# Attention kernel on one NeuronCore: the block maxima turned on VectorE in 32x32 squares, the group statistics summed as fp32r records, and GpSimd held at two places

## The chip, the cores and the metric

The kernel runs on one core of a Trainium2 chip. The metric is the device time of one execution in microseconds (us), lower is better. The kernel before was timed three times; its median is 1215.44 us (1214.12 to 1215.74).

## The reference, cut to what matters

The input x has 16 images of 64x64 positions and 256 channels (n = 4096 positions per image). Every operation is in float32.

```python
xg  = group_norm(x)                      # 32 groups of 8 channels, eps 1e-5
qkv = xg @ W_qkv                         # 256 -> 768, split in q, k, v
k   = softmax(k, over the 4096 positions)
ctx = einsum('bdn,ben->bde', k, v)       # 256 x 256
out = einsum('bde,bdn->ben', ctx, q)
y   = x + out @ W_out + b_out
```

The softmax runs over the positions of an image, so it needs a maximum for each of the 256 channels of k.

## The kernel before, in words

The work goes image by image, b = 0 to 15, and an image in 8 chunks j of 512 positions; a chunk has 4 tiles of 128 positions. `n` is b + 1. Each float32 product is made of three fp32r products: every operand is split in a rounded part (`_hi`, written by ScalarE) and a rest (`_lo`, a subtraction on VectorE or GpSimd).

For one image the program does this.
- **Statistics.** `bn_half` (VectorE, L849) reads chunks of the image after the next; `bn_sum` (L851) gives mean and variance of each channel. `stats_mean` (TensorE, L462) multiplies the 128 means by `grp`, a 128x128 matrix of 1/8 inside each group of 8 channels, in float32; `mean_of` (VectorE, L860 to L865) subtracts, and forms each channel's share of the variance; `stats_var` (L466) sums that with the same matrix; `var_of` (L871) adds eps; `rstd_of` (GpSimd, L357) takes the power -0.5. These small steps for image n are placed in the first two steps of the gather of image b.
- **Keys.** `keys` (L399) makes `ps_k` for each chunk; `keys_out` (ScalarE, L685) copies it to `e_raw`; `key_max` (VectorE, L889 and L892) keeps in `mx` [128 x 256] the maximum over tiles, of one block of four chunks (blk 0: j = 0 to 3; blk 1: j = 4 to 7). A row of `mx` is a position modulo 128, a column a channel.
- **The maximum of a block.** `turn_max` (TensorE, L447) transposes the two halves of `mx` into PSUM; `block_max` (VectorE, L901) reduces them to `m_blk` [128 x 2], a channel in each partition; `spread_max` (TensorE, L455) multiplies `m_blk`, broadcast along 128 columns, by the identity in float32, which puts the 256 maxima in every partition of PSUM; `shift` (VectorE, L917) subtracts them from `e_raw`. `block_scales` (L906, L909) gives `dm`, the difference of the block's maximum to that of the image, and ScalarE takes its exponential, `alpha`.
- **Exponentials and gather.** `exps` (ScalarE, L693 and L699) makes `e_hi` and the exact exponential, `e_low` (VectorE, L924) the rest. `gather_high` (TensorE, L480 and L482: 16 matmuls) and `gather_low` (L492: 8) multiply chunk j of the exponentials by the chunk of x.
- **Combine and emit.** `combine_u`, `combine_m` and `bias_sum` (L542) form one 256x256 matrix and a bias; `emit` (L564, L573) applies it to all chunks of x of the image, between the `keys` of image n.

The order on every engine is written out by hand, one queue each. TensorE begins the gather of image b with `gather_high(b, 0)`, then `turn_max(b, 1)`, `stats_mean(n)`, `gather_low(b, 0)`, `gather_high(b, 1)`, `spread_max(b, 1)`, `stats_var(n)`, `gather_low(b, 1)` (L619 to L628; in image 0 the two statistics come after the gathers of chunks 3 and 4). For block 0 of image n, `turn_max(n, 0)` and `spread_max(n, 0)` stand around `keys(n, 4)` (L661 to L666). VectorE's order is in `gather_steps` (L1053) and in `period` (L1100 to L1121). GpSimd (L372) makes `xt_lo` (`xt_low`, L341) and `x_lo` (`x_low`, L347), each 128x1024, as soon as ScalarE has the rounded part; the first of a period is `xt_low(n, 0)`.

Two places in the code that the prediction speaks of:

```python
# VectorE, before: gather_steps
block_max(b, 1)
if more:
    mean_of(n, np_)
block_scales(b)
```

```python
# GpSimd, before: the start of a period
if more:
    xt_low(n, np_, 0)
    if b:
        rstd_of(n, np_)
for j in range(HALF, NCH):
    x_low(b, j)
```

## Time and profile before

| | |
|---|---|
| median of three runs | 1215.44 us |
| the profiled execution | 1214.93 us, its span 1213.2 us |
| TensorE (PE) busy | 1190.1 us, 98% of the span |
| VectorE (DVE), ScalarE (ACT), GpSimd (POOL) busy | 69%, 69%, 51% |
| granted TensorE clock | 1.00 throughout |
| data moved by DMA | 219 GB/s over the span |

The span is cut from the first to the last instruction; 1.7 us of the execution lie outside it. A matmul row of the timeline shows when the first of a group starts and how long the group runs to its modelled end; matmuls are pipelined, so what one costs is read from the distance of starts, not from its duration. PE is TensorE, DVE VectorE, ACT ScalarE, POOL GpSimd.

### The profile page before, as it was taken

The page shows a single profiled execution, that of the slowest core. Times are in us where ns is not written, and L with a number is a line of the kernel's source. Part 1 is how long each engine was busy: PE and PEld are TensorE (multiplying, and loading weights), DVE is VectorE, ACT ScalarE, POOL GpSimd, SP SyncE. Part 2 cuts the span into 40 slices and gives each one's busy share as a digit, 9 for nine tenths or more (in the row PEclk, how much of TensorE's full clock was granted, in tenths as well). Part 3 has the DMA queues.
Part 4 walks back from the last instruction along what each step waited for, and adds up shares of the span by engine and source line. Part 5 has one row for each costly group of instructions (what it writes and reads, how often), then busy time and mean ns, then how long its engine had stood idle before and what let it go on. Part 6 is the DMA issues. An engine that isn't in the chain of part 4 may idle for free.

```text
span 1213.2 us, 21447 instructions
## 1 busy us (share of the span) xinstructions
PE 1190.1 (98%) x8460; PEld 1115.8 (92%) x8460; DVE 842.1 (69%) x1582; ACT 840.1 (69%) x1140; POOL 622.4 (51%) x288
## 2 busy tenths in 40 slices
PE   4999999999999999999999999999999999999998
PEld 4998999999899998999989999899999989999897
DVE  6877667676776767768776677766767676676551
ACT  5767768677685776757677686776857768577664
POOL 8664564635645355563655636356463564536520
PEclk9999999999999999999999999999999999999999
DMA  9448666576765758666486665867657576573524
GB/s 339 146 167 294 218 235 205 195 269 208 274 203 199 264 172 294 226 206 237 162 301 229 221 227 183 286 209 252 204 201 263 193 278 225 201 252 122 191 74 170
DMA packets 107077, 266.71 MB, mean 220 GB/s; under 512 B 10208, under 2 KB 10208, under 8 KB 106976
## 3 DMA queue, kind: packets, MB, share of 16 engines
q1 hardware_dynamic: 106976, 265.33, 63.5%
q8 instruction: 67, 1.10, 0.4%
q14 instruction: 34, 0.28, 0.1%
HBM read 198.18 MB, written 67.11 MB: 219 GB/s over the span
## 4 chain that ended last, share of the span: by engine, by line
PE 93%; DVE 2%; ACT 1%; POOL 1%; DMA 1%; issue 1%; SPq 0%; DVEq 0%; POOLq 0%; ACTq 0%
PE ps_k L399 29%; PE ps_e L564 19%; PE ps_e L573 10%; PE ps_g L492 5%; PE ps_e L480 5%; PE ps_e L492 5%; PE ps_e L482 5%; PE ps_g L480 4%; PE ps_g L482 4%; PE ps_g L511 1%; PE ps_g L528 1%; PE ps_g L542 1%; PE ps_g L534 1%; POOL x_lo L347 1%; DVE mx L892 1%
## 5 line engine op out<-in xcount | busy, mean ns | idle before, releaser
L341 POOL TENSOR_TENSOR xt_lo<-xt_raw,xt_hi 128x1024 fp32r<-128x1024 f32 x128 | 307.4, 2404 | 434.5 <-ACT xt_hi L676 309.1
L347 POOL TENSOR_TENSOR x_lo<-x_raw,x_hi 128x1024 fp32r<-128x1024 f32 x128 | 281.4, 2216 | 65.6 <-ACT x_hi L681 56.2
L892 DVE TENSOR_TENSOR mx<-ps_k,mx 128x256 f32<-128x256 f32 x480 | 203.3, 424 | 95.8 <-ACT e_raw L685 74.3
L733 ACT ACTIVATE o_stage<-ps_e,bias 128x512 f32<-128x512 f32 x253 | 170.9, 689 | 114.1 <-PE ps_e L573 114.1
L399 PE MATMUL ps_k<-wk_hi,xt_hi 128*128 128x256 f32 x1024 | 207.1, 284 | 1.0 <-DVE mx L892 0.7
L399 PE MATMUL ps_k<-wk_lo,xt_hi 128*128 128x256 f32 x1024 | 205.5, 283 | 0.0
L685 ACT ACTIVATE e_raw<-ps_k 128x512 f32<-128x512 f32 x256 | 141.4, 596 | 87.2 <-PE ps_k L399 87.2
L849 DVE BATCH_NORM_STATS2 bn<-xs 128x6 f32<-128x512 f32 x240 | 154.5, 686 | 40.7 <-DMA xs<-in_xt_dram 39.5
L693 ACT ACTIVATE e_hi<-e_raw 128x1024 fp32r<-128x1024 f32 x128 | 135.1, 1055 | 60.9 <-DVE e_raw L917 33.0
L399 PEld LDWEIGHTS ps_k<-wk_hi,xt_hi 128*128 128x128 f32 x1024 | 163.4, 190 | 8.7 <-issue 1.8
L399 PE MATMUL ps_k<-wk_hi,xt_lo 128*128 128x256 f32 x1024 | 158.2, 283 | 0.0
L399 PEld LDWEIGHTS ps_k<-wk_lo,xt_hi 128*128 128x128 f32 x1024 | 157.4, 189 | 0.0
L564 PE MATMUL ps_e<-xt_hi,acc_hi 128*128 128x512 f32 x474 | 150.3, 398 | 0.0
L573 PE MATMUL ps_e<-xt_hi,u_lo 128*128 128x512 f32 x474 | 150.2, 398 | 0.0
L564 PE MATMUL ps_e<-xt_lo,acc_hi 128*128 128x512 f32 x474 | 148.8, 395 | 0.0
L681 ACT ACTIVATE x_hi<-x_raw 128x1024 fp32r<-128x1024 f32 x128 | 134.5, 1050 | 11.4 <-DMA x_raw<-in_xn_dram 11.2
L676 ACT ACTIVATE xt_hi<-xt_raw 128x1024 fp32r<-128x1024 f32 x128 | 135.0, 1055 | 3.8 <-DMA xt_raw<-in_xt_dram 3.8
L399 PEld LDWEIGHTS ps_k<-wk_hi,xt_lo 128*128 128x128 f32 x1024 | 137.3, 189 | 0.0
L480 PE MATMUL ps_e<-x_hi,e_hi 128*128 128x258 f32 x512 | 125.8, 283 | 0.7 <-POOL x_lo L347 0.7
L482 PE MATMUL ps_e<-x_lo,e_hi 128*128 128x256 f32 x512 | 125.5, 282 | 0.0
L482 PE MATMUL ps_g<-x_lo,e_hi 128*128 128x256 f32 x512 | 124.8, 281 | 0.0
L480 PE MATMUL ps_g<-x_hi,e_hi 128*128 128x258 f32 x512 | 124.8, 282 | 0.0
(129 smaller groups left out, 1992.7 us busy)
## 6 DMA issues: line engine op xcount, KB each, us to landing
xt_raw<-in_xt_dram SPq DMA_DIRECT2D x128, 512.0 KB, 4.3
x_raw<-in_xn_dram SPq DMA_DIRECT2D x128, 512.0 KB, 3.5
out_dram<-o_stage SPq DMA_DIRECT2D x127, 512.0 KB, 4.5
xs<-in_xt_dram SPq DMA_DIRECT2D x240, 256.0 KB, 5.1
w_setup<-in_w_dram SPq DMA_DIRECT2D x2, 256.0 KB, 10.1
out_dram<-o_stage SPq DMA_DIRECT2D x2, 256.0 KB, 2.0
wk<-in_w_dram SPq DMA_DIRECT2D x1, 256.0 KB, 9.9
wq_t<-in_w_dram SPq DMA_DIRECT2D x1, 256.0 KB, 10.9
```

The costliest lines, as they stand in the source:

```text
L341: nc.gpsimd.tensor_tensor(xt_lo[:, s], xt_raw[:, s], xt_hi[:, s].bitcast(F32), ALU.subtract).then_inc(xt_lo_ready, 1)
L347: nc.gpsimd.tensor_tensor(x_lo[:, s], x_raw[:, s], x_hi[:, s, :, 0:C].bitcast(F32), ALU.subtract).then_inc(x_lo_ready, 1)
L399: return nc.tensor.matmul(ps_k[:, j % 2, t // 2, (t % 2) * C:(t % 2 + 1) * C], (xt_hi, xt_lo)[xs_][:, slot(j, parity), c, t * P:(t + 1) * ...
L480: nc.tensor.matmul(ps_g[j // HALF][:, d, 0:C + 2], w_, x_hi[:, j % X_SLOTS, t, :], start=(j % HALF == 0 and t == 0), stop=False, skip_grou ...
L482: nc.tensor.matmul(ps_g[j // HALF][:, d, 0:C], w_, x_lo[:, j % X_SLOTS, t, :], start=False, stop=False, skip_group_check=True)
L564: nc.tensor.matmul(out_psum(b, u, h), hi[:, c, h * P:(h + 1) * P], x_[:, s, c, :], start=(n == 0 and c == 0), stop=False, skip_group_check ...
L573: last = nc.tensor.matmul(out_psum(b, u, h), lo[:, c, h * P:(h + 1) * P], xt_hi[:, s, c, :], start=False, stop=(c == CB - 1), skip_group_c ...
L685: nc.scalar.activation(e_raw[:, j, 2 * h:2 * h + 2, :].rearrange("p t c -> p (t c)"), ps_k[:, j % 2, h, :], ACT.Copy).then_inc(k_out, 1)
L693: nc.scalar.activation(e_hi[:, j % E_SLOTS], e_raw[:, j], ACT.Exp).then_inc(e_hi_ready, 1)
L733: nc.scalar.activation(o_stage[:, u % O_SLOTS, h, :], src, ACT.Identity, bias=bias[:, h:h + 1]).then_inc(o_ready, 1)
L849: nc.vector.bn_stats(bn[:, q % CB, q // CB, :], xs[:, q % S_SLOTS, :]).then_inc(bn_done, 1)
L892: nc.vector.tensor_tensor(mx[:], tile, mx[:], ALU.max).then_inc(max_done, 1)
```

## The change

- VectorE turns `mx` with its own transpose, which works in squares of 32x32 (`turned`). A reduction over each square's 32 columns gives `quad` [128 x 8]; three moves bring the other three groups of 32 partitions beside the first; a last reduction gives `m_blk`, now 32 partitions x 8. `turn_max` is gone from TensorE. The moves are written as a `tensor_reduce` of single elements (`move`), not as copies.
- `block_diag` (VectorE) splits `m_blk` in a rounded part and a rest in `m_parts` (64 partitions), and multiplies it by two stacked 32x32 identities into `diag`, 64x256 fp32r. `spread_max` is now one fp32r matmul of 256 columns with ones as weights.
- The group sums of images 1 to 15 use `grp_r` and parts (rounded, rest) in fp32r: one matmul of 4 columns in place of a float32 one of 2. VectorE forms the parts (`mean_parts`, `var_parts`) and adds the two sums afterwards. In `mean_of`, `dev` is now the sum of `mv` and `neg_mean`, both in SBUF; before, it read the mean from PSUM.
- `alpha` is made from 32 partitions (`alpha_q`) and spread by four moves in `spread_scales`.
- GpSimd waits for `diag_ready` of block 1 before `xt_low(n, 0)`, and for that of block 0 before `xt_low(n, 5)`.
- ScalarE makes the fp32r copies of `grp` and of the ones, and `eye2`, before its first work.

```diff
             def period(b, parity, more, more2):
                 n, np_ = b + 1, 1 - parity
+                pool.wait_ge(diag_ready, b * 2 + 2)
                 if more:
                     xt_low(n, np_, 0)
...
                     for j in range(3, NCH):
+                        if j == HALF + 1:
+                            pool.wait_ge(diag_ready, n * 2 + 1)
                         xt_low(n, np_, j)
...
-            def turn_max(b, blk):
-
-                to = max_psum(b, blk)
-                pe.wait_ge(max_done, b * (TILES * NCH) + TILES * HALF * (blk + 1))
-                for d in range(CB):
-                    last = nc.tensor.transpose(to[:, 0, d * P:(d + 1) * P], mx[:, d * P:(d + 1) * P], ident)
-                last.then_inc(t_ps, 1)
-
             def spread_max(b, blk):
-                to = max_psum(b, blk)
-                pe.wait_ge(m_blk_ready, b * 2 + (blk + 1))
-                for d in range(CB):
-                    last = nc.tensor.matmul(to[:, 1, d * P:(d + 1) * P],
-                                            m_blk[:, blk, d:d + 1].broadcast_to([P, P]), ident,
-                                            start=(d == 0), stop=True, skip_group_check=True)
-                last.then_inc(bc_ps, 1)
+                pe.wait_ge(diag_ready, b * 2 + (blk + 1))
+                nc.tensor.matmul(max_psum(b, blk)[:, 1, 0:C], one_r[0:2 * Q].broadcast_to([2 * Q, P]), diag,
+                                 start=True, stop=True).then_inc(bc_ps, 1)
...
+                    pe.wait_ge(mean_parts_ready, b)
+                    nc.tensor.matmul(stats_psum(b, 0), grp_r[:], mean_parts[:].rearrange("p k c -> p (k c)"), start=True,
+                                     stop=True).then_inc(mean_ps, 1)
...
+                    pe.wait_ge(var_parts_ready, b)
+                    nc.tensor.matmul(stats_psum(b, 1), grp_r[:], var_parts[:].rearrange("p k c -> p (k c)"), start=True,
+                                     stop=True).then_inc(var_ps, 1)
...
             def mean_of(b, parity):
                 dve.wait_ge(mean_ps, b + 1)
...
+                    nc.vector.tensor_scalar(mean_rest[:], sums[:, CB:2 * CB], -1.0, None,
+                                            ALU.mult).then_inc(mean_rest_ready, 1)
+                    dve.wait_ge(mean_rest_ready, b)
+                    nc.vector.scalar_tensor_tensor(out=neg_mean[:, parity, :], in0=sums[:, 0:CB], scalar=-1.0,
+                                                   in1=mean_rest[:], op0=ALU.mult, op1=ALU.add).then_inc(mean_sum_ready, 1)
+                    dve.wait_ge(mean_sum_ready, b)
+                    nc.vector.tensor_tensor(dev[:], mv[:, :, 0], neg_mean[:, parity, :], ALU.add).then_inc(mean_read, 1)
...
+                if b > 0:
+                    dve.wait_ge(var2_ready, b + 1)
+                    move(var_parts[:, 0, :], var2[:]).then_inc(var_hi_ready, 1)
+                    dve.wait_ge(var_hi_ready, b)
+                    nc.vector.tensor_tensor(var_parts[:, 1, :], var2[:], var_parts[:, 0, :].bitcast(F32),
+                                            ALU.subtract).then_inc(var_parts_ready, 1)
...
             def block_max(b, blk):
-                src = max_psum(b, blk)
-                dve.wait_ge(t_ps, b * 2 + (blk + 1))
-                nc.vector.tensor_reduce(m_blk[:, blk, :], src[:, 0, 0:C].rearrange("p (d n) -> p d n", d=CB),
-                                        AX_X, ALU.max).then_inc(m_blk_ready, 1)
+                n = b * 2 + blk + 1
+                dve.wait_ge(max_done, n * (TILES * HALF))
+                nc.vector.transpose(turned[:], mx[:]).then_inc(turned_ready, 1)
+                dve.wait_ge(turned_ready, n)
+                nc.vector.tensor_reduce(quad[:, :, 0], turned[:].rearrange("p (q k) -> p q k", k=Q), AX_X,
+                                        ALU.max).then_inc(quad_ready, 1)
+                dve.wait_ge(quad_ready, n)
+                for r in range(1, QUADS):
+                    last = move(quad[0:Q, :, r], quad[r * Q:(r + 1) * Q, :, 0])
+                last.then_inc(quad_moved, 1)
+                dve.wait_ge(quad_moved, n)
+                nc.vector.tensor_reduce(m_blk[:, blk, :], quad[0:Q], AX_X, ALU.max).then_inc(m_blk_ready, 1)
+
+            def block_diag(b, blk):
+                n = b * 2 + blk + 1
+                dve.wait_ge(m_blk_ready, n)
+                move(m_parts[0:Q, :], m_blk[:, blk, :]).then_inc(m_part_hi_ready, 1)
+                dve.wait_ge(m_part_hi_ready, n)
+                nc.vector.tensor_tensor(m_parts[Q:2 * Q, :], m_blk[:, blk, :], m_parts[0:Q, :].bitcast(F32),
+                                        ALU.subtract).then_inc(m_part_lo_ready, 1)
...
+                dve.wait_ge(m_part_lo_ready, n)
+                nc.vector.tensor_tensor(diag.rearrange("p (q k) -> p q k", k=Q),
+                                        eye2[:].unsqueeze(1).broadcast_to([2 * Q, NQ, Q]),
+                                        m_parts[:].bitcast(F32).unsqueeze(2).broadcast_to([2 * Q, NQ, Q]),
+                                        ALU.mult).then_inc(diag_ready, 1)
```

TensorE at the start of the gather of an image (b from 1 to 14), the 16 matmuls of `gather_high` on either side left out. Before:

```order
L447 MATMUL ps_k<-zero_eye,mx 128x128 x2
L462 MATMUL ps_k<-mv,grp 128x2
...
L455 MATMUL ps_k<-zero_eye,m_blk 128x128 x2
L466 MATMUL ps_k<-var,grp 128x2
```

And changed:

```order
L499 MATMUL ps_k<-mean_parts,grp_r 128x4
...
L488 MATMUL ps_k<-u_hi,one_r 128x256
L509 MATMUL ps_k<-var_parts,grp_r 128x4
```

The positions are the same, the two transposes are gone, and each float32 matmul has become one fp32r matmul (`u_hi` is the memory that `diag` lies in).

VectorE at the same place, from the last `e_low` ahead of the gather to the first `shift` of block 1. Before:

```order
L924 TENSOR_TENSOR e_lo<-e_raw,e_hi 128x1024
L901 TENSOR_REDUCE m_blk<-ps_k 128x2
L860 TENSOR_TENSOR dev<-mv,ps_k 128x2
L861 TENSOR_SCALAR neg_mean<-ps_k 128x2
L865 TENSOR_SCALAR var<-dev,mv 128x1 x2
L906 TENSOR_REDUCE m_all<-m_blk 128x2
L909 TENSOR_TENSOR dm<-m_blk,m_all 128x4
L961 TENSOR_TENSOR b_mean<-b_col,neg_mean 128x2
L917 TENSOR_TENSOR e_raw<-e_raw,ps_k 128x1024
```

And changed, up to `dm`:

```order
L985 STREAM_TRANSPOSE turned<-mx 128x256
L987 TENSOR_REDUCE quad<-turned 128x8
L890 TENSOR_REDUCE quad<-quad 32x8 x3
L994 TENSOR_REDUCE m_blk<-quad 32x8
L890 TENSOR_REDUCE m_parts<-m_blk 32x8
L1001 TENSOR_TENSOR m_parts<-m_blk,m_parts 32x8
L1006 TENSOR_TENSOR u_hi<-eye,m_parts 64x256
L924 TENSOR_SCALAR mean_rest<-ps_k 128x2
L927 SCALAR_TENSOR_TENSOR neg_mean<-ps_k,mean_rest 128x2
L930 TENSOR_TENSOR dev<-mv,neg_mean 128x2
L933 TENSOR_SCALAR var<-dev,mv 128x1 x2
L890 TENSOR_REDUCE var_parts<-var 128x2
```

One instruction ahead of `mean_of` has become nine, and the chain from the mean to the part that `stats_var` reads has grown from four instructions to seven; the last of them (L940, `var_parts`) and `dm` follow.

## Rows read from the trace of the kernel before

**Rows 1.** The page, busy time of each engine over the span.
```profile
PE 1190.1 (98%) x8460; PEld 1115.8 (92%) x8460; DVE 842.1 (69%) x1582; ACT 840.1 (69%) x1140; POOL 622.4 (51%) x288
```
**Rows 2.** What TensorE waited for: total us, times, longest.
```profile
PE ps_k L447 <- DVE mx L892: 1.9, 2, 1.6
...
PE ps_e L480 <- POOL x_lo L347: 0.7, 2, 0.4
```
**Rows 3.** Timeline of PE, start of image 1's gather: start us, us, operation, count.
```profile
123.21 0.28 PE L480 MATMUL ps_g<-x_hi,e_hi 128*128 128x258 f32 x1
...
125.12 0.38 PE L447 MATMUL ps_k<-zero_eye,mx 128*128 128x128 f32 x2
...
128.44 0.60 PE L455 MATMUL ps_k<-zero_eye,m_blk 128*128 128x128 f32 x4
...
130.08 0.28 PE L480 MATMUL ps_g<-x_hi,e_hi 128*128 128x258 f32 x1
...
132.95 0.28 PE L480 MATMUL ps_g<-x_hi,e_hi 128*128 128x258 f32 x1
```
**Rows 4.** Timeline of PE, around `keys(2, 4)`, and `keys(2, 3)` before it.
```profile
168.75 0.40 PE L399 MATMUL ps_k<-wk_hi,xt_hi 128*128 128x256 f32 x2
...
172.10 0.63 PE L564 MATMUL ps_e<-xt_lo,acc_hi 128*128 128x512 f32 x2
...
174.43 0.38 PE L447 MATMUL ps_g<-zero_eye,mx 128*128 128x128 f32 x2
...
177.49 0.61 PE L455 MATMUL ps_g<-zero_eye,m_blk 128*128 128x128 f32 x4
...
178.41 0.63 PE L564 MATMUL ps_e<-xt_lo,acc_hi 128*128 128x512 f32 x2
```
**Rows 5.** PE groups by form: `bias_sum`'s records, 128 of one column.
```profile
L542 PE MATMUL ps_g<-neg_mean,acc 128*128 128x1 f32 x128 | 15.2, 239 | 0.0
```
**Rows 6.** Timeline of DVE at the start of image 1's gather.
```profile
122.62 1.21 DVE L924 TENSOR_TENSOR e_lo<-e_raw,e_hi 128x1024 fp32r<-128x1024 f32 x1
...
125.95 0.15 DVE L861 TENSOR_SCALAR neg_mean<-ps_k 128x2 f32<-128x2 f32 x1
126.14 0.46 DVE L865 TENSOR_SCALAR var<-dev,mv 128x1 f32<-128x1 f32 x2
...
126.69 0.85 DVE L909 TENSOR_TENSOR dm<-m_blk,m_all 128x4 f32<-128x4 f32 x1
```
**Rows 7.** DVE groups by form, one operation over 256 columns.
```profile
L889 DVE COPY mx<-ps_k 128x256 f32<-128x256 f32 x32 | 13.5, 421 | 2.4 <-PE ps_e L447 1.4 <-ACT e_raw L685 1.0
...
L901 DVE TENSOR_REDUCE m_blk<-ps_k 128x2 f32<-128x256 f32 x16 | 6.8, 424 | 23.9 <-PE ps_k L447 23.9
```
**Rows 8.** Timeline of POOL at the start of image 1's gather.
```profile
125.12 2.40 POOL L341 TENSOR_TENSOR xt_lo<-xt_raw,xt_hi 128x1024 fp32r<-128x1024 f32 x1 [7.79 <-ACT xt_hi L676]
```
**Rows 9.** Line L909 (`dm`): duration ns min/median/max of its 16.
```profile
L909 DVE TENSOR_TENSOR dm<-m_blk,m_all x16: 161/833/849, 52.0 to 1158.7; 128x4 f32<-128x4 f32 x16
```
**Rows 10.** Timeline of DVE, the maxima of `keys(2, 3)`.
```profile
171.98 1.87 DVE L892 TENSOR_TENSOR mx<-ps_k,mx 128x256 f32<-128x256 f32 x4 [2.79 <-ACT e_raw L685]
```
**Rows 11.** Timeline of POOL beside it.
```profile
173.46 2.42 POOL L341 TENSOR_TENSOR xt_lo<-xt_raw,xt_hi 128x1024 fp32r<-128x1024 f32 x1 [3.19 <-ACT xt_hi L676]
```
**Rows 12.** Timeline of POOL, image 0: two `first_e_low`.
```profile
49.88 4.77 POOL L352 TENSOR_TENSOR e_lo<-e_raw,e_hi 128x1024 fp32r<-128x1024 f32 x2 [1.43 <-ACT e_raw L699]
```
**Rows 13.** Timeline of DVE, image 0: `shift(0, 3)` and `e_low(0, 3)`.
```profile
50.24 1.21 DVE L917 TENSOR_TENSOR e_raw<-e_raw,ps_e 128x1024 f32<-128x1024 f32 x1
...
55.31 2.79 DVE L924 TENSOR_TENSOR e_lo<-e_raw,e_hi 128x1024 fp32r<-128x1024 f32 x1
```
**Rows 14.** Timeline of PE, image 0: `spread_max(0, 1)`.
```profile
53.53 0.60 PE L455 MATMUL ps_k<-zero_eye,m_blk 128*128 128x128 f32 x4
```
**Rows 15.** Timeline of DVE, image 15: the last `e_low` before its gather.
```profile
1156.95 1.22 DVE L924 TENSOR_TENSOR e_lo<-e_raw,e_hi 128x1024 fp32r<-128x1024 f32 x1
```
**Rows 16.** Timeline of PE, image 15: `gather_low(15, 1)`, behind `spread_max(15, 1)`.
```profile
1160.60 1.21 PE L492 MATMUL ps_g<-x_hi,e_lo 128*128 128x258 f32 x8
```

More of the change, by code:

```diff
@@ L29 @@
 POOL_LOW = 3
+Q = 32
+QUADS = P // Q
 def build(nc: bass.Bass, xt: bass.AP, xn: bass.AP, w: bass.AP, b_out: bass.AP, out: bass.AP):
@@ L93, in build @@
         eye = [zero_eye[:, P:3 * P], zero_eye[:, 0:2 * P]]
-        grp = sb("grp", [P, P])
+        with nc.sbuf_tensor("grp", [P, P], F32) as grp:
+            pass
+        grp_r = sb("grp_r", [P, P], F32R)
+        one_r = sb("one_r", [P, 1], F32R)
+        var_sum = sb("var_sum", [P, CB])
+        var_parts = sb("var_parts", [P, 2, CB], F32R)
+        mean_parts = sb("mean_parts", [P, 2, CB], F32R)
+        mean_rest = sb("mean_rest", [P, CB])
         mx = sb("mx", [P, C])
@@ L107, in build @@
         u_lo = sb("u_lo", [P, CB, C], F32R)
+        with nc.sbuf_tensor("turned", [P, C], F32) as turned:
+            pass
         u_hi = sb("u_hi", [P, CB, C], F32R)
+        diag = u_hi[0:2 * Q, 1, :]
         m_lo = u_lo
@@ L213, in stats_psum @@
         def stats_psum(b, which):
-            return ps_k[:, 0, 0, C + which * CB:C + (which + 1) * CB] if b == 1 else ps_k[:, 1, which, 0:CB]
+            if b == 1:
+                return ps_k[:, 0, 0, C + 2 * CB * which:C + 2 * CB * (which + 1)]
+            return ps_k[:, 1, which, 0:CB if b == 0 else 2 * CB]
         def max_psum(b, blk):
@@ new lines, in stats_mean @@
+            def stats_mean(b):
+                if b == 0:
+                    pe.wait_ge(mv_ready, 1)
+                    nc.tensor.matmul(stats_psum(b, 0), grp_r[:].bitcast(F32), mv[:, :, 0], start=True,
+                                     stop=True).then_inc(mean_ps, 1)
+                else:
+                    pe.wait_ge(max_done, b * (TILES * NCH))
+                    pe.wait_ge(mean_parts_ready, b)
+                    nc.tensor.matmul(stats_psum(b, 0), grp_r[:], mean_parts[:].rearrange("p k c -> p (k c)"), start=True,
+                                     stop=True).then_inc(mean_ps, 1)
@@ new lines, in stats_var @@
+            def stats_var(b):
+                if b == 0:
+                    pe.wait_ge(var2_ready, 1)
+                    nc.tensor.matmul(stats_psum(b, 1), grp_r[:].bitcast(F32), var2[:], start=True,
+                                     stop=True).then_inc(var_ps, 1)
+                else:
+                    pe.wait_ge(var_parts_ready, b)
+                    nc.tensor.matmul(stats_psum(b, 1), grp_r[:], var_parts[:].rearrange("p k c -> p (k c)"), start=True,
+                                     stop=True).then_inc(var_ps, 1)
@@ L739, in emit @@
                         emit_half(b, u, h)
+            act.wait_ge(consts_ready, 5)
+            nc.scalar.activation(grp_r[:], grp[:], ACT.Copy).then_inc(grp_r_ready, 1)
+            nc.scalar.activation(one_r[:], one_col[:], ACT.Copy).then_inc(one_r_ready, 1)
+            for r in range(2):
+                last = nc.scalar.activation(eye2[r * Q:(r + 1) * Q, :], ident[r * Q:(r + 1) * Q, r * Q:(r + 1) * Q],
+                                            ACT.Copy)
+            last.then_inc(eye2_ready, 1)
             for j in range(NCH):
@@ L908, in block_scales, with spread_scales @@
                 dve.wait_ge(m_all_ready, b + 1)
-                nc.vector.tensor_tensor(dm[:], m_blk[:], m_all[:].unsqueeze(1).broadcast_to([P, 2, CB]),
+                nc.vector.tensor_tensor(dm[:], m_blk[:], m_all[:].unsqueeze(1).broadcast_to([Q, 2, NQ]),
                                         ALU.subtract).then_inc(dm_ready, 1)
+            def spread_scales(b):
+                dve.wait_ge(alpha_q_ready, b + 1)
+                by_quad = alpha_q[:].rearrange("p k (d r) -> p k d r", r=QUADS)
+                for r in range(QUADS):
+                    last = move(alpha[r * Q:(r + 1) * Q, :, :], by_quad[:, :, :, r])
+                last.then_inc(alpha_ready, 1)
             def shift(b, j):
@@ L1020, in _ @@
             bn_half(1, 10)
+            block_max(0, 0)
+            block_diag(0, 0)
             key_maxes(0, 4)
-            block_max(0, 0)
             bn_half(1, 11)
@@ L1044, in first_gather @@
                 mean_of(1, 1)
+                spread_scales(0)
                 take_first(0)
@@ L1055, in gather_steps @@
                 block_max(b, 1)
+                block_diag(b, 1)
                 if more:
@@ L1065, in gather_steps @@
                 e_low(b, 4)
+                spread_scales(b)
                 take_first(b)
```

73 lines of the change are left out of this document (55 added, 18 removed).

## Prediction

> **What bounds the kernel now.** I read the page's busy times first: TensorE is busy 98% of the span, the next engines 69% [rows 1]. Then its waits: it waited for no engine for longer than 1.6 us at once, and in the steady images it did not wait at all; the waits that I use lie in images 0, 1 and 15 [rows 2]. So matmul time taken away shortens the span one for one, as long as nothing that TensorE waits for becomes late. What can become late is on VectorE and GpSimd, so I read last the timelines of the places where the change works. The reader is to see there when VectorE has a result, and when TensorE comes for it.
>
> **What TensorE loses.** Each price is a distance between starts. At the start of a gather, from `gather_high(b, 0)` at 123.21 to `gather_high(b, 2)` at 130.08 are 6.87 us. One chunk with nothing between is 132.95 - 130.08 = 2.87 us, two are 5.74, so turn, mean, spread and variance cost 1.13 us [rows 3]. They become three matmuls. A record of one column in `bias_sum` costs 15.2 / 128 = 0.12 us [rows 5], and a full one in `gather_high` (123.21 to 125.12, 16 of them) also 0.12 [rows 3]; three are 0.36. Saved: 0.77 us. At block 0, turn to the second emit row are 178.41 - 174.43 = 3.98 us, the same work without turn and spread 172.10 - 168.75 = 3.35 [rows 4]: 0.63 us become 0.12, saved 0.51. Images 1 to 14 have the first place with statistics, images 1 to 15 the second: 14 x 0.77 + 15 x 0.51 = **18.4 us off**. Images 0 and 15 are counted below.
>
> **What VectorE gets, at the start of a gather.** Its work there begins when the last `e_low` is out, 122.62 + 1.21 = 123.8 [rows 6]. The turn, the reduction and the product for `diag` have 256 columns each, 0.42 us, and 0.03 more before the next can start: 1.35 us. I have no row of a transpose; the copy and the reduction of the same size agree [rows 7], the ends are 0.35 and 0.9. Six small ones remain (three moves, the last maximum, rounded part, rest). A small one that depends on the one before starts 0.19 us after it (125.95, then 126.14) [rows 6]; two independent small ones start 0.07 apart. The moves are independent, but each reads another quarter of the partitions, so I give them the long distance: six at 0.18 are 1.08, and 0.85 if the moves overlap. `diag` is ready at 123.8 + 2.43 = 126.2. TensorE, 0.2 us earlier without the turn, comes for it after chunk 0, the mean and the first 16 of chunk 1, at 123.21 + 2.87 + 0.12 + 1.91 = 128.1, so `spread_max` is covered by 1.9 us.
>
> The Trainium skill (VectorE: DVE Perf Modes, section on two Vector instructions with no wait between them) says that an instruction starts only after all earlier ones if its input begins in another quadrant of partitions than the last one read. By that rule the moves cannot overlap and `diag` is at 126.2; by the short distance it would be at 126.0 and the sum 3 us lower.
>
> **The wait that comes in its place.** `dm` has four columns and takes 0.16 us at the least, but 0.83 in the median [rows 9]. In image 1 it starts at 126.69 and ends at 127.54; GpSimd's `xt_low(n, 0)` runs from 125.12 to 127.52 [rows 6, 8]. In image 0 `e_low(0, 3)` takes 2.79 us for 1.21, under GpSimd as well [rows 13]. Both have two SBUF inputs. `neg_mean` and the variance steps, with PSUM or one tensor, ran at normal length in the same window [rows 6]. So a VectorE operation with two SBUF inputs stands still until GpSimd's instruction ends. Before the change `dev` read PSUM and escaped this. Now `dev` and the rest for `var_parts` have two SBUF inputs each. And the new wait releases `xt_low(n, 0)`, whose input is ready at 125.1 [rows 8], just when `diag` is ready: it runs from 126.3 to 128.7, while `dev` comes 0.5 us after `diag`. `dev` ends at 128.7, the two variance steps take 0.50, rounded part and rest 0.36, the signal 0.04: `var_parts` at 129.6. TensorE comes for it behind the spread at 128.1 + 0.12 = 128.2. It stands 1.4 us, and the whole queue behind it. If `dev` slips in before GpSimd, the rest is caught instead and the wait is 1.0; with overlapping moves 1.1; with a turn of 0.9 us 1.8. Fourteen images: **19.6 us on** (14.0 to 25).
>
> After that nothing more is late: by the same distances `shift(b, 4)` follows 0.8 us later than before and TensorE itself 0.5, and the 0.3 between them is covered by the two chunks of gather that lie ahead of the first use (2 x 2.87 us); without them it would be added to the wait. `spread_scales` (four moves, 0.7 us at most) stands where VectorE waits for the gather of chunk 3; were that wait gone, the first copy of the sums would be 0.7 us later.
>
> **Block 0.** The maxima end at 171.98 + 1.87 = 173.85 [rows 10]. GpSimd's `xt_low(2, 4)` runs until 175.88 [rows 11] and holds the rest for `m_parts` until then, which is due two big and five small distances after the maxima, at 175.65; `diag` is at 176.5, TensorE comes at 177.49 - 0.18 = 177.3 [rows 4]. No cost. The hold of `xt_low(n, 5)` moves it to 176.6, and `keys(2, 5)` stand behind the next emit: nothing.
>
> **Image 0.** `shift(0, 3)` ends at 51.45 [rows 13]; the chain reaches the rest at 53.25, where the second `first_e_low` holds it until 49.88 + 4.77 = 54.65 [rows 12]. `diag` is at 55.3, `spread_max(0, 1)` stood at 53.53 [rows 14]: 1.7 us late. Then `xt_low(1, 0)` starts and holds `dm`, and `shift(0, 4)`, the remaining `bn_half` and `mean_parts` are 4 to 5 us late; followed through the queues this adds up to 5.5 us on TensorE's queue by chunk 7, 2 if `dm` slips in first. I take **4.5 us on**. The fills of ScalarE at the start fit in its wait for the first data, and block 0 there costs at most 0.3.
>
> **Image 15.** The last emits stand elsewhere, so TensorE comes early. `e_low` ends at 1158.17 [rows 15], `diag` 2.4 later at 1160.6, when `gather_low(15, 1)` started before [rows 16]: no gain, no loss.
>
> **Sum.** -18.4 + 19.6 + 4.5 = +5.7 us on the profiled execution of 1214.93, that is 1220.6 us; against the median, which is 0.5 higher, the same change would give 1221.1. I say 1220.5.
>
> **The rivals.**
> - *VectorE's small operations are not held.* If the 0.83 of `dm` had another cause, `var_parts` would come seven small distances after `diag`, at 127.5, and be hidden behind TensorE's 128.2. Only image 0 costs 1 to 2 us. 1214.9 - 18.4 + 1.5 = 1198. For it: nothing but that the rows show just two operations held. Against it: both ends agree with GpSimd's to 0.02 us.
> - *The wait is short.* Overlapping moves, `dev` ahead of GpSimd and image 0 at 2 us: 1214.9 - 18.4 + 14 x 0.9 + 2 = 1211. It decides as soon as the wait per image is below 1.15 us, where faster begins.
> - *Block 0 is late too.* If the transpose or the reduction is also held by GpSimd, the chain at block 0 starts at 175.9, `diag` is at 178.3, and TensorE stands 1.0 us in 15 images: 1235. The trace has no transpose; operations with one tensor, as the variance steps in the window of [rows 8], were not held [rows 6], so I give this little.
> - *The hold does nothing.* If GpSimd's input came later than `diag`, the new waits would be idle; here it is ready 1.1 us earlier, so they act.
>
> **How the numbers follow.** My forecast, with its own range of 1214 to 1227, has 0.57. Unheld operations have 0.13, the short wait 0.17, block 0 late 0.09, anything else 0.04. The range 1206 to 1229 leaves out the first rival and most of the third, and takes in the second with both ends of the moves. A change under 0.2% (2.4 us) could not be told from none. Faster (below 1213.0): the first two rivals and a little of the rest, 0.32. Same: the low end of my case, 0.16. Slower: 0.52.
>
> **What the changed profile would show.** TensorE's waits would have a new first line, `stats_var`'s matmul waiting for VectorE's L940 some 14 times with 1.4 us each. `dev` (L930) would last until GpSimd's `xt_low` ends, 2.2 us in place of 0.15. `spread_max` would wait only in images 0 and 15. TensorE's span between the gathers of two images would stay near 74.0 us, 1.3 less in matmuls and as much more in waits. I am wrong if L930 has its normal length, or if `spread_max` waits in every image.

## The result, and the profile after

The changed kernel takes 1228.64 us (median of 4 runs, 1227.95 to 1229.39) against 1215.44 for the one before (median of three; a fourth run of it took 4129.46 us and is left out): the ratio is 1.0112, with an interval from 1.0092 to 1.0131. It is slower by 13 us, where the prediction said 5. The profiled execution has a span of 1226.8 us, 13.6 more than before, and all further sums are made on the spans.

The page's busy line of the changed kernel, against [rows 1]:

```profile
PE 1183.1 (96%) x8270; PEld 1102.2 (90%) x8270; DVE 940.4 (77%) x1992; ACT 842.0 (69%) x1144; POOL 621.6 (51%) x288
```

TensorE lost 7.0 us of busy time and 190 instructions, and yet the span grew. VectorE is busy for 98 us more; part of this is standing still, as the timeline below shows.

What TensorE waited for in the changed kernel (total us, times, longest):

```profile
PE ps_k L509 <- DVE var_parts L940: 15.6, 14, 1.1
PE ps_k L488 <- DVE u_hi L1006: 4.4, 2, 3.5
```

The first row is new: 14 waits of 1.1 us at `stats_var`. The second has an unusual longest wait, 3.5 us, in image 0. Before, the longest for this block maximum was 1.6 us, at `turn_max` [rows 2].

The timeline of VectorE at the start of image 1's gather, to be held against [rows 6]:

```profile
128.94 1.22 DVE L1039 TENSOR_TENSOR e_lo<-e_raw,e_hi 128x1024 fp32r<-128x1024 f32 x1
130.08 0.43 DVE L985 STREAM_TRANSPOSE turned<-mx 128x256 f32<-128x256 f32 x1
130.55 0.42 DVE L987 TENSOR_REDUCE quad<-turned 128x8 f32<-128x256 f32 x1
131.00 0.50 DVE L890 TENSOR_REDUCE quad<-quad 32x8 f32<-32x8 f32 x3
...
131.93 0.16 DVE L1001 TENSOR_TENSOR m_parts<-m_blk,m_parts 32x8 fp32r<-32x8 f32 x1
132.12 0.42 DVE L1006 TENSOR_TENSOR u_hi<-eye,m_parts 64x256 fp32r<-64x256 f32 x1
...
132.64 0.16 DVE L927 SCALAR_TENSOR_TENSOR neg_mean<-ps_k,mean_rest 128x2 f32<-128x2 f32 x1
132.84 2.20 DVE L930 TENSOR_TENSOR dev<-mv,neg_mean 128x2 f32<-128x2 f32 x1
135.07 0.46 DVE L933 TENSOR_SCALAR var<-dev,mv 128x1 f32<-128x1 f32 x2
135.56 0.15 DVE L890 TENSOR_REDUCE var_parts<-var 128x2 fp32r<-128x2 f32 x1
135.75 0.16 DVE L940 TENSOR_TENSOR var_parts<-var,var_parts 128x2 fp32r<-128x2 f32 x1
```

And of GpSimd beside it, against [rows 8]:

```profile
132.62 2.40 POOL L381 TENSOR_TENSOR xt_lo<-xt_raw,xt_hi 128x1024 fp32r<-128x1024 f32 x1 [8.93 <-DVE u_hi L1006]
```

The chain from the end of `e_low` (130.16) to that of `diag` (132.54) takes 2.4 us. GpSimd starts at 132.62, 0.08 us behind `diag`. `dev`, of two columns, starts at 132.84 and ends at 135.04, and GpSimd's operation ends at 135.02. `neg_mean` (L927) also has two tensors, but one lies in PSUM: it ran in 0.16 us, although it started at 132.64, 0.02 us behind GpSimd. The kernel before shows this more plainly: its `dev`, with one tensor in PSUM, started 0.76 us behind GpSimd [rows 8] in image 1, and all 16 of them, each under an operation of GpSimd, took 0.15 to 0.16 us.

```profile
125.88 0.15 DVE L860 TENSOR_TENSOR dev<-mv,ps_k 128x2 f32<-128x2 f32 x1
```

The variance steps, the rounded part and the rest follow at normal length.

The timeline of TensorE at the same place, against [rows 3]:

```profile
129.50 0.28 PE L524 MATMUL ps_g<-x_hi,e_hi 128*128 128x258 f32 x1
...
131.39 0.17 PE L499 MATMUL ps_k<-mean_parts,grp_r 128*128 128x4 f32 x1
...
134.47 0.38 PE L488 MATMUL ps_k<-u_hi,one_r 64*128 64x256 f32 x1
135.97 0.27 PE L509 MATMUL ps_k<-var_parts,grp_r 128*128 128x4 f32 x1 [1.12 <-DVE var_parts L940]
...
137.14 0.28 PE L524 MATMUL ps_g<-x_hi,e_hi 128*128 128x258 f32 x1
```

From `gather_high(1, 0)` at 129.50 to `gather_high(1, 2)` at 137.14 are 7.64 us, before 6.87. The wait of 1.12 us took more than the 0.77 that was saved.

The timeline of TensorE around the spread of block 0, from `keys(2, 4)` at 180.84 to the second emit row at 184.66, against [rows 4]:

```profile
180.84 0.39 PE L442 MATMUL ps_k<-wk_hi,xt_hi 128*128 128x256 f32 x2
...
182.73 1.11 PE L442 MATMUL ps_k<-wk_hi,xt_lo 128*128 128x256 f32 x8
183.77 0.38 PE L488 MATMUL ps_g<-u_hi,one_r 64*128 64x256 f32 x1
184.08 0.74 PE L608 MATMUL ps_e<-xt_hi,acc_hi 128*128 128x512 f32 x2
184.66 0.62 PE L608 MATMUL ps_e<-xt_lo,acc_hi 128*128 128x512 f32 x2
```

The whole is 3.82 us long. Without any spread it was 3.35, so `spread_max` costs 0.47 us here. The float32 turn and spread together cost 0.63.

**Where the 13.6 us are.** I cut the spans at the matmul of `stats_mean` at the start of a gather (125.34 before, 131.39 after). Thirteen images further on it is at 1087.14 and at 1099.61. This gives three pieces: 6.1 us up to the first cut, 6.4 us in the thirteen images, 1.1 us behind them. The median distance of one image grew from 73.94 to 74.45 us.

Within an image, two places changed, and in each kernel each of them takes the same time in all images to 0.03 us. At the start of a gather (first matmul of chunk 0 to that of chunk 2, 14 images) the median was 6.85 us and is 7.64. At block 0 (the last emit row ahead of `keys(n, 4)` to the second one behind the spread, 15 images) it was 4.44 and is 4.29.

Of the 6.1 us, 1.0 lies ahead of image 0's `stats_mean` (15.33 before, 16.35 after) and 4.6 between it and that of image 1. The first is a DMA chunk that landed late; of the experiments, two started at 15.5 and the others at 16.0 to 16.6, so these runs cannot tell it from chance. The second is image 0. Two views show it, first VectorE's timeline:

```profile
54.60 1.38 DVE L1001 TENSOR_TENSOR m_parts<-m_blk,m_parts 32x8 fp32r<-32x8 f32 x1
56.02 0.42 DVE L1006 TENSOR_TENSOR u_hi<-eye,m_parts 64x256 fp32r<-64x256 f32 x1
...
56.55 2.36 DVE L1016 TENSOR_TENSOR dm<-m_blk,m_all 32x16 f32<-32x16 f32 x1
```

and TensorE's `spread_max(0, 1)`, which stood at 53.53 before [rows 14]:

```profile
56.49 0.58 PE L488 MATMUL ps_k<-u_hi,one_r 64*128 64x256 f32 x1 [3.47 <-DVE u_hi L1006]
```

The granted clock changed here as well. The windows of the changed kernel behind this wait (us; busy time of PE, PEld, DVE, ACT, POOL; then the granted TensorE clock, DMA share, GB/s).

```profile
56.00:58.00 2.00, 1.51 (x5) 1.28 (x6) 1.94 (x3) 1.80 (x2) 1.48 (x1) 0.50 0.00 0
58.00:60.00 2.00, 2.00 (x12) 2.00 (x11) 2.00 (x4) 0.21 (x1) 2.00 (x2) 0.50 0.00 0
60.00:62.00 2.00, 2.00 (x11) 2.00 (x11) 2.00 (x3) 0.67 (x1) 1.04 (x1) 0.50 0.72 262
62.00:64.00 2.00, 2.00 (x16) 2.00 (x16) 1.96 (x6) 2.00 (x3) 0.00 (x0) 0.83 0.00 0
```

TensorE stood for 3.47 us, from 53.0 to 56.5, and its granted clock was 0.50, the 1.2 GHz level, from 55.9 to 62.7. Before, the same stretch has 1.00 throughout.

### The profile page after: what moved, and what is told of

The parts are those of the page before. It is cut to its first block, busy times and chain, and to the rows that moved or that the text cites. A ratio compares the mean times of both kernels' runs of the same rounds, so it can differ in the third digit from the quotient of the medians.

```text
span 1226.8 us, 21528 instructions
## 1 busy us (share of the span) xinstructions
PE 1183.1 (96%) x8270; PEld 1102.2 (90%) x8270; DVE 940.4 (77%) x1992; ACT 842.0 (69%) x1144; POOL 621.6 (51%) x288
## 4 chain that ended last, share of the span: by engine, by line
PE 78%; DVE 13%; ACT 4%; DMA 2%; issue 1%; POOL 1%; SPq 0%; DVEq 0%; POOLq 0%; ACTq 0%
PE ps_k L442 24%; PE ps_e L608 17%; PE ps_e L617 9%; PE ps_e L524 5%; PE ps_e L536 5%; PE ps_e L526 5%; PE ps_g L536 4%; DVE mx L974 3%; DVE dev L930 3%; PE ps_g L524 2%; PE ps_g L526 2%; DVE e_lo L1039 2%; DMA xs<-in_xt_dram 1%; ACT e_raw L741 1%; PE ps_g L555 1%
## 6 DMA issues: line engine op xcount, KB each, us to landing
wq_t<-in_w_dram SPq DMA_DIRECT2D x1, 256.0 KB, 11.1
```

## The experiments

All of them start from the changed kernel. Each was timed beside the kernel before on the same chip (1215.4, 1215.5, 1215.1 and 1214.8 us in the four sets). "Per image" is the median distance between the cuts defined above (73.94 before, 74.45 after), "thirteen" the sum of the thirteen (961.8 and 968.2).

### The wait at the variance

Theory: `dev` stands under GpSimd, and this makes the 14 waits. Its alternative: the chain is long because it has more instructions. **Pointer operand** leaves all steps, but gives `dev` and the rest of `var_parts` one tensor and a per-partition scalar in place of two tensors. That makes two instructions of each, so the chain becomes longer, not shorter.

```diff
-nc.vector.tensor_tensor(dev[:], mv[:, :, 0], neg_mean[:, parity, :], ALU.add)
+for c in range(CB):
+    last = nc.vector.tensor_scalar(dev[:, c:c + 1], mv[:, c, 0:1], neg_mean[:, parity, c:c + 1], None, ALU.add)
```

(the same for the subtraction that writes `var_parts[:, 1]`)

> The changed kernel with dev and the rest of var_parts formed as subtractions with a per-partition scalar, two instructions of one column in place of one with two SBUF tensors. Theory 'GpSimd holds the operation with two SBUF tensors': dev takes 0.15 us per column in place of 2.20, TensorE no longer waits for var_parts (15.6 us of waits gone, and with the restart about 1.2 us in each of 14 images), so about 17 us less than the changed kernel: 1211 to 1213 us. Rival 'the chain itself is too long, the held operation only uses slack': the wait shrinks by less than half, 1220 us or more.

Measured: 1214.21 us, ratio 0.9995 (0.9986 to 1.0005), 73.27 per image. Its groups on VectorE (busy us, mean ns) and TensorE's wait at the variance:

```profile
L931 DVE TENSOR_SCALAR dev<-mv,neg_mean 128x1 f32<-128x1 f32 x30 | 5.0, 210 | 0.5
L944 DVE TENSOR_SCALAR var_parts<-var,var_parts 128x1 fp32r<-128x1 f32 x30 | 5.0, 210 | 0.5
```

```profile
PE ps_k L509 <- DVE var_parts L944: 0.4, 1, 0.4
```

The time is 1.2 us above the range that was expected. Neither operation is held now, the wait is down from 15.6 us to 0.4, and 14.4 us are gone from the median. The number of instructions was not the cause. The gain against before is 0.67 us per image, about half of the 1.28 that the prediction counted.

**Float32 statistics** undoes the other half of the change instead: `grp` and the sums in float32, no parts, `dev` reading PSUM again; the transposes in squares, the diagonal and GpSimd's waits stay.

```diff
-    pe.wait_ge(mean_parts_ready, b)
-    nc.tensor.matmul(stats_psum(b, 0), grp_r[:], mean_parts[:].rearrange("p k c -> p (k c)"), start=True, stop=True)
+    pe.wait_ge(mv_ready, b + 1)
+    nc.tensor.matmul(stats_psum(b, 0)[:, 0:CB], grp_r[:].bitcast(F32), mv[:, :, 0], start=True, stop=True)
```

(in sense; likewise for the variance and for VectorE's side)

> The changed kernel with the group statistics undone: float32 matmuls of two columns, dev read from PSUM, no parts; the maxima on VectorE, the diagonal and GpSimd's waits stay. Theory 'the fp32r statistics are what brought the held operations': no wait for the variance, two float32 records cost 0.2 us more than two fp32r ones, so a steady image at 73.4 to 73.6 us and about 1215 us, 13 us less than the changed kernel. Rival 'the held operation is not the point, the longer VectorE chain at the diagonal is': the wait for the variance stays above 0.8 us and the time above 1222 us.

Measured: 1214.48 us, ratio 0.9990 (0.9980 to 0.9999), 73.52 per image. TensorE no longer waits at the variance of any image but the first. `dev` has one operand in PSUM again and, without the two steps ahead of it, starts at 129.79 in image 1, 0.15 us before GpSimd. Its group:

```profile
L923 DVE TENSOR_TENSOR dev<-mv,ps_k 128x2 f32<-128x2 f32 x16 | 2.3, 143 | 0.7 <-PE ps_k L496 0.7
```

So there are two ways out of the wait with the same result, and the fp32r records themselves are worth 73.52 - 73.27 = 0.25 us per image.

### What the spread costs

The changed `spread_max` is a matmul over 64 rows (`64*128` in its row) among others over 128. Theory: the change of shape costs time. Rivals: fetching the new weights, or the arithmetic of 256 columns. **Spread over 128 rows** fills the diagonal, `m_parts` and `eye2` up with zeros, so the sum is the same and the matmul has the shape of its neighbours.

```diff
-diag = u_hi[0:2 * Q, 1, :]
+diag = u_hi[:, 1, :]
-nc.tensor.matmul(max_psum(b, blk)[:, 1, 0:C], one_r[0:2 * Q].broadcast_to([2 * Q, P]), diag,
+nc.tensor.matmul(max_psum(b, blk)[:, 1, 0:C], one_r[:].broadcast_to([P, P]), diag,
```

> The changed kernel with the spread matmul over 128 rows in place of 64 (the added 64 rows of the diagonal are zero, the same VectorE instruction writes them). Theory 'a matmul of 64 rows among those of 128 costs extra because the array changes its shape': the distance keys(n, 4) to the second emit row falls from 3.82 us to about 3.5, 15 times 0.3 at block 0, while at block 1 the wait for var_parts takes back what is gained: about 1224 us. Rival 'a matmul with broadcast ones as weights or 256 columns of the diagonal is dear in itself': no change, 1228.6 us.

TensorE's timeline at the spread of block 0 of image 2, where in the changed kernel 1.04 us lay ahead of the spread's start and 0.89 behind it, up to the second emit row:

```profile
183.92 1.11 PE L442 MATMUL ps_k<-wk_hi,xt_lo 128*128 128x256 f32 x8
184.87 0.28 PE L488 MATMUL ps_g<-u_hi,one_r 128*128 128x256 f32 x1
184.99 0.62 PE L608 MATMUL ps_e<-xt_hi,acc_hi 128*128 128x512 f32 x2
185.45 0.62 PE L608 MATMUL ps_e<-xt_lo,acc_hi 128*128 128x512 f32 x2
```

Here it is 0.95 and 0.58 us, together 0.40 less, and over 15 images block 0 takes 3.89 us in place of 4.29. With twice the rows the matmul became cheaper. Yet the whole kernel is hardly faster: 1225.99 us, ratio 1.0083 (1.0066 to 1.0100). The wait at the variance took up what was gained at the start of a gather:

```profile
PE ps_k L509 <- DVE var_parts L942: 18.8, 15, 1.4
```

It was 15.6 us, 1.1 at the most; the start of a gather takes 7.66 us, as before this edit 7.64. The saving at block 0 shows in the median image, 74.08, but four of the thirteen took 75.0 to 75.5, and in this run TensorE waited four times, 3.7 us in all, for ScalarE's `o_stage`, which the changed kernel never did.

**Spread twice** issues the same 64-row matmul a second time right behind itself.

```diff
+nc.tensor.matmul(max_psum(b, blk)[:, 1, 0:C], one_r[0:2 * Q].broadcast_to([2 * Q, P]), diag,
+                 start=True, stop=True)
```

> The changed kernel with the spread matmul of 64 rows issued twice in a row (the second overwrites the first with the same values). Theory 'change of shape': the second one needs no change and adds 0.12 to 0.2 us at block 0, about 2 us in all, 1231 us. Rival 'dear in itself': each adds 0.3 to 0.45 us, 15 times at block 0, 1233 to 1236 us.

```profile
182.76 1.11 PE L442 MATMUL ps_k<-wk_hi,xt_lo 128*128 128x256 f32 x8
183.79 0.38 PE L488 MATMUL ps_g<-u_hi,one_r 64*128 64x256 f32 x1
184.01 0.28 PE L490 MATMUL ps_g<-u_hi,one_r 64*128 64x256 f32 x1
184.22 0.73 PE L610 MATMUL ps_e<-xt_hi,acc_hi 128*128 128x512 f32 x2
184.79 0.64 PE L610 MATMUL ps_e<-xt_lo,acc_hi 128*128 128x512 f32 x2
```

The timeline (same place) shows 1.00 us from the first spread to the second emit row, in place of 0.89. A second one of the same kind adds 0.11, the price of any 256-column matmul, so the 0.4 us are paid once, at the change from 128 rows to 64 and back. The time was 1231.92 us (1.0139, 1.0124 to 1.0154), 74.53 per image. The distance per image grew by only 0.08. The span grew by 2.9 us, 1.8 in the thirteen images (most of it one image of 75.94) and 1.1 behind them; what made these two, the run does not show.

The Trainium skill (TensorEngine Tiling (Array Packing), Key Properties) says that changing the tiling mode, of which one has 64 rows, drains TensorE. The three runs agree with it, though none shows the array itself; the page has no duration, and 0.40 us is what the rows give.

**Both** puts the pointer operand and the 128 rows together.

> Per-partition scalars in place of the two held operations, and the spread matmul over 128 rows. If both causes are real and separate, the pitch of a steady image falls from 73.27 us (scalars alone) by twice 0.4 us to about 72.5, in all 11 us less than 1214.2: about 1203 us. Rival 'what one gives back another wait takes': the wait for images' first diagonal or for o_stage grows, pitch above 73.0, 1210 us or more.

Measured: 1206.44 us, ratio 0.9925 (0.9907 to 0.9942), thirteen images 947.5. At the start of a gather there is now nothing between the spread and the variance:

```profile
134.95 0.28 PE L488 MATMUL ps_k<-u_hi,one_r 128*128 128x256 f32 x1
135.07 0.17 PE L509 MATMUL ps_k<-var_parts,grp_r 128*128 128x4 f32 x1
```

0.12 us, where the pointer kernel has 0.31. The two places of an image, in the medians defined above, show what each cause was worth:

| | start of a gather | block 0 |
|---|---|---|
| before | 6.85 us | 4.44 us |
| changed | 7.64 | 4.29 |
| pointer operand | 6.44 | 4.29 |
| spread over 128 rows | 7.66 | 3.89 |
| both | 6.06 | 3.88 |

The two causes add up, and the gains that the prediction counted, 0.77 and 0.51 us, are there once both are out of the way: 0.79 and 0.56. The best images take 72.45 us, 1.49 less than before, the median one 72.8. The expected 72.5 and 1203 us were missed by 0.3 and 3 us: four of the thirteen images took 73.4 to 73.8, and TensorE waited 3 times for `o_stage` and twice for `x_lo`, 3.4 us in all.

### GpSimd's two waits

**Hold later** keeps GpSimd until the parts of the variance are ready.

```diff
-                pool.wait_ge(diag_ready, b * 2 + 2)
+                if more and b:
+                    pool.wait_ge(var_parts_ready, n)
+                else:
+                    pool.wait_ge(diag_ready, b * 2 + 2)
```

> The changed kernel with GpSimd released before xt_low(n, 0) by var_parts_ready of image n (for image 0 by the diagonal, as in the change). Nothing is computed otherwise. Theory 'held': dev has its short length because GpSimd rests, var_parts comes about 1.3 us after the diagonal, TensorE's wait for it is gone, 1211 to 1213 us like the kernel with the per-partition scalars. Rival 'GpSimd's xt_lo or x_lo then come late': TensorE waits for x_lo or xt_lo by up to 1 us per image, 1220 us or more.

Measured: 1215.37 us, ratio 1.0004 (0.9994 to 1.0013), 73.42 per image. `dev` in its group, and `dm` (min/median/max):

```profile
L933 DVE TENSOR_TENSOR dev<-mv,neg_mean 128x2 f32<-128x2 f32 x15 | 2.6, 172 | 0.5
```

```profile
L1019 DVE TENSOR_TENSOR dm<-m_blk,m_all x16: 161/2391/2399, 56.1 to 1160.1; 32x16 f32<-32x16 f32 x16
```

The same instruction as in the changed kernel, with two tensors and 128x2, takes 0.17 us when GpSimd starts later. `dm` is the next with two SBUF inputs and now stands for 2.4 us; TensorE shows no new wait for it. This excludes every cause of the 2.20 us that lies in `dev` itself. The time is 2.4 us above the expected range, and an image takes 0.15 us more than with the pointer operand; the run does not show where.

**No hold** takes both waits of GpSimd away and nothing else.

> The changed kernel without GpSimd's two waits for the diagonal. xt_low(n, 0) then starts when its input is there, about 0.9 us before VectorE's rest for m_parts is due, and holds it until about 133.8 in image 1 (diagonal 1.9 us later); dev is free afterwards. Theory 'held': the wait moves from var_parts to the diagonal and to var_parts together and stays near 1.2 to 1.5 us per image; 1226 to 1231 us, so the holds as placed are worth next to nothing. Rival 'the holds are what protects': each image loses the 2 us of the diagonal on top, 1245 us or more. Rival 'the holds are what hurts': below 1220 us.

Measured: 1226.96 us, ratio 1.0096 (1.0081 to 1.0111), 1.7 less than with the waits, with intervals that overlap. Image 1 on VectorE, and GpSimd:

```profile
134.66 1.92 DVE L998 TENSOR_TENSOR m_parts<-m_blk,m_parts 32x8 fp32r<-32x8 f32 x1
...
137.33 0.16 DVE L927 TENSOR_TENSOR dev<-mv,neg_mean 128x2 f32<-128x2 f32 x1
```

```profile
134.17 2.39 POOL L381 TENSOR_TENSOR xt_lo<-xt_raw,xt_hi 128x1024 fp32r<-128x1024 f32 x1 [7.19 <-ACT xt_hi L715]
```

GpSimd's operation ends at 136.56, the rest for `m_parts` at 136.58. Now this one stands for 1.9 us and `dev` for nothing. TensorE's wait at the variance is 11.5 us in place of 15.6, that for `diag` in image 0 5.6 in place of 3.5. In the changed kernel the holds do nothing but choose which instruction of one chain stands still. From this alone they seem to be worth nothing; the next run asks the same of the good version.

**Both, without the holds** is the kernel of 1206.4 us without GpSimd's two waits.

> The changed kernel with both repairs (the difference and the rest for the variance through a per-partition scalar, spread_max over 128 rows) and without GpSimd's two new waits; everything is computed. If the waits on GpSimd protect the diagonal's chain (theory of the change), the rest for m_parts is now caught by GpSimd for about 1.9 us at the start of each gather, spread_max comes late, and the kernel is slower than the one with both repairs and the waits (1206.4 us) by 5 us or more. If the chain has slack enough in the steady images (my reading: diag has 1.9 us in hand at the start of a gather), only image 0 and small shifts change: within 2.5 us of 1206.4, with the rest for m_parts (L1001 or near it) at 1.9 us in the median, and the diagonal's wait of TensorE in total 5 to 7 us.

Measured: 1226.24 us, ratio 1.0096 (1.0079 to 1.0113). My reading fell: the holds are worth 20 us there. VectorE and TensorE at the start of image 1's gather, and the total of the wait:

```profile
133.03 1.88 DVE L1005 TENSOR_TENSOR m_parts<-m_blk,m_parts 32x8 fp32r<-32x8 f32 x1
134.94 0.42 DVE L1010 TENSOR_TENSOR u_hi<-eye,m_parts 128x256 fp32r<-128x256 f32 x1
```

```profile
135.45 0.36 PE L485 MATMUL ps_k<-u_hi,one_r 128*128 128x256 f32 x1
137.11 0.27 PE L506 MATMUL ps_k<-var_parts,grp_r 128*128 128x4 f32 x1 [1.30 <-DVE var_parts L943]
```

```profile
PE ps_k L506 <- DVE var_parts L943: 18.2, 14, 1.3
```

I had been right about `diag`: it is ready at 135.36, just ahead of TensorE at 135.45. But `dev` and the variance stand in the same queue behind it, and `stats_var` comes 0.12 us after the spread. The rest for `m_parts` lost 1.7 us, and TensorE stands for 1.3 of them one matmul later, 14 times. Both waits were taken away together, so no run gives the share of each; but these 18.2 us all lie at the start of a gather, where the first of them stands, and at block 0 TensorE waited for no diagonal. From these two pairs of kernels, a hold pays when everything behind it, up to the last result that TensorE takes, is free of operations that GpSimd can catch.

### Image 0, and the best version

In image 0 GpSimd's own work ahead of the hold catches the rest for `m_parts` (above, 54.60). **Scales first** is "both" with image 0's `block_scales` moved ahead of its `block_diag`, so that `dm` is done before GpSimd's next operation is released.

```diff
                 block_max(0, 1)
-                block_diag(0, 1)
                 block_scales(0)
                 mean_bias(0, 0)
+                block_diag(0, 1)
```

> As the kernel with both changes, and in image 0 the block scales stand ahead of the diagonal on VectorE, so that dm is not held by xt_low(1, 0). Theory 'in image 0 the held dm makes the shifts late': the wait for e_lo (1.8 us) in image 0 and the second fall of the clock at 70 to 80 us are gone, 2 to 3 us less than with both changes alone: about 1200 us. Rival 'the diagonal of image 0 counts, and it becomes 0.3 us later': no gain or up to 1 us worse.

Measured: 1204.47 us, ratio 0.9910 (0.9895 to 0.9925). TensorE's wait for the diagonal is still there, 3.8 us at the longest; `dm` was not in its way. What the theory named did change, by the one profile of each kernel: the wait for `e_lo` is 1.0 us in place of 1.8, the granted clock does not fall a second time (1.00 from 70 to 80 us, where "both" has 0.83), and from image 0's `stats_mean` to image 2's there are 113.9 us in place of 115.9. The first fall lasted 6.8 us, though, in place of 3.4, and the intervals of the two times meet, so the gain of 2 us is likely and not shown.

**Diagonal early** moves image 0's `block_max` and `block_diag` in front of `shift(0, 3)` in "both".

> Both changes (scalars, 128 rows), and in image 0 the maximum and the diagonal of block 1 stand ahead of shift(0, 3) on VectorE. Theory 'the first diagonal costs image 0 its 5 us, and with them the clock': the rest for m_parts is due just before GpSimd's first e_low ends and not in the middle of the second, the diagonal comes some 2 us earlier, TensorE's wait of 3.5 us becomes 1.5 us and the granted clock does not fall to half behind it; about 3 us less than 1206.4: 1202 to 1204 us. Rival 'exps(0, 3) or the later shifts bound image 0': 1206 us or more, with a new wait for e_hi or e_lo.

Measured: 1204.69 us, ratio 0.9915 (0.9901 to 0.9929). The wait for the diagonal is 3.3 us at the longest, no better than 3.5: the rest now passed (53.64, 0.15 us), and the product for `diag`, which also has two SBUF inputs, took 2.46 us in place of 0.42. So this diagonal came no earlier to speak of, and the granted clock fell both times as in "both". The intervals of this and the last kernel overlap.

**Float32 statistics, 128 rows, scales first** asks whether the fp32r statistics are worth the eight small instructions that an image has for them on VectorE (2022 in all against 1902).

> Statistics in float32 as before the change, the maxima on VectorE, the spread matmul over 128 rows, and in image 0 the scales ahead of the diagonal. From the kernel with float32 statistics (1214.5 us, 73.52 us per image): twice 0.4 us less per image, 72.7 us, 1203 us. Theory 'the fp32r records give back no more than 0.2 us per image': this is within 3 us of the kernel with scalars and 128 rows (1206.4 and 1204.5 us). Rival 'they are worth keeping': this is slower by more than 4 us.

Measured: 1204.57 us, ratio 0.9913 (0.9899 to 0.9926), thirteen images 948.6 against 947.3 with records. So the total does not show the 0.25 us per image: in these kernels no chain of VectorE sets the pace, but some images take 73.2 to 74.0 in place of 72.45, with short waits for `x_lo` and `o_stage` in the trace (5 and 3 times, 3.6 us in all with the records). What holds these images back in full was not settled.

All three beat the kernel before by 0.9%. The simplest is the last, which needs neither parts nor sums of parts.

## Why the prediction was right and wrong

**Right: the mechanism, its place and its sign.** A VectorE operation with two SBUF inputs stands until GpSimd's ends. The prediction had it from `dm` [rows 8, 9] and `e_low(0, 3)` [rows 13], and named `dev` as the victim, with 2.2 us, released by the new hold. It measured 2.20, and the wait was 1.1 us in all 14 images where 1.4 were forecast. The runs bear it out from three sides: a scalar operand or a later GpSimd lets `dev` through, and without the hold the stall moves to `m_parts`. `dev` before and `neg_mean` after, with one input in PSUM, ran under GpSimd at full speed. The Trainium skill (SBUF — State Buffer, SBUF: two separate sides) calls the ports that both engines share an exclusive lock that is held for the whole instruction. The end of `dev` 0.02 us behind GpSimd's agrees. One reading of the waits was incomplete: the longest, 15.3 us for the first data at the start, is left out of "no engine for longer than 1.6 us"; nothing in the sum rests on it.

**Right: the lengths.** The transpose of 256 columns took 0.44 us where 0.42 was assumed, and the chain up to `diag` took 2.4 us against 2.43. The three moves took 0.50 us, 0.17 apart and not 0.07, which agrees with the rule that the prediction weighed (the Trainium skill, VectorE: DVE Perf Modes, section on two Vector instructions with no wait between them). The first rival (nothing is held, 1198) is excluded by `dev`. The third (block 0 late) too: without the hold the transpose of image 2's block 0, at 182.76, took 0.45 us though GpSimd was at work from 182.33 to 184.73, and TensorE waited for a diagonal in only two images.

**Wrong, and the step that failed: the price of the new `spread_max`, "They become three matmuls ... three are 0.36" and, at block 0, "0.63 us become 0.12".** The price of 0.12 us came from rows in which a matmul follows others of its own shape [rows 3, 5]. The new spread has 64 rows and they have 128. Its change of shape stood in the sum at nothing; it costs 0.35 to 0.4 us each time, and the spread 0.47 in all at block 0. So block 0 saved 0.15 us, not 0.51. At the start of a gather the same loss (6.44 - 6.06 = 0.38 in the runs without the wait) lies ahead of the wait and is mostly covered by it, which is why the wait is 1.1 us and not 1.4; the stretch as a whole took 0.79 us more, where the prediction's own terms give 1.4 - 0.77 = 0.63.

**Image 0: near by luck.** Forecast 4.5 us; the cuts give 4.6 up to image 1's `stats_mean`, and 0.4 up to image 2's although block 0 saved 0.15 there and the start of image 1's gather 0.24 ahead of the cut, so 5.4. The forecast had `diag` 1.7 us late, and the wait was 3.5: GpSimd's second `first_e_low` ended at 55.97 and not at 54.65, and TensorE reached the spread at 53.0 and not at 53.53. The fall of the granted clock to 0.50 for 6.8 us was not in it at all. That the sums are so near is luck: what made up for both in the queues behind was not followed.

| term | forecast, us | measured, us |
|---|---|---|
| start of a gather, 14 times | 14 x 0.63 = 8.8 | 14 x 0.79 = 11.1 |
| block 0, 15 times | -15 x 0.51 = -7.7 | -15 x 0.15 = -2.3 |
| elsewhere in thirteen images | 0 | 13 x (0.51 - 0.64) = -1.7 |
| image 0 | 4.5 | 5.4 |
| ahead of image 0 | 0 | 1.0 |
| rest behind the last cut | 0 | 1.1 - 0.79 - 0.24 + 0.15 = 0.2 |
| sum | 5.7 | 13.7 (span: 13.6) |

Most of the miss is the second line, where nothing covers the dearer spread: 5.4 of the 8 us. Another 2.3 are the first line. The 0.13 us per image that went elsewhere are there in the pointer kernel and in "both" too (0.11 and, in the best images, 0.14); I did not find where. The rival of a short wait (1211) came near the wait of 1.1 us for none of its reasons: the moves did not overlap, `dev` did not slip in ahead of GpSimd, and image 0 cost 5.4 us and not 2. Its limit of 1.15 us does not follow from its own sum either: 1214.9 - 18.4 + 14 x wait + 2 falls below 1213.0 at 1.03.

## What to carry to other kernels

Price a matmul with the change of shape that it brings: one over fewer rows than its neighbours cost 0.47 us here where the full one cost 0.07, and zeros in the missing rows are cheaper than the change. Before an instruction of GpSimd is released at a point, list what VectorE has queued behind that point with two SBUF inputs: the first of them takes the stall, and a per-partition scalar or an operand in PSUM avoids it. Judge a hold only with the rest of its chain free: the same two waits were worth nothing that the intervals show in one kernel (-1.7 us) and 20 us in the next.
